# Single rows fetched by byte offsets kept in the sorted records, read 32 registers at a time, in a graph network kernel

## The reference, cut to what matters

```python
x = x + attention(h, src, dst, ...)
msg = xw[et_all, src_all]                       # layer 2: one of 8 x 12500 rows per edge and direction
out = sum over types of segment_sum(msg) * deg_inv + h @ self_weight
h2 = h[dst] + edge_attr_16 @ W_edge + b_edge    # layer 3, with the node itself as one more edge
agg = segment_sum(h2, src)
messages = (h @ W + b)[src] + edge_attr_6 @ We + be   # layer 4
x = x + relu(segment_sum(messages, dst))
```

## Time and profile before

| what | before |
|---|---|
| median of three timed runs | 21862.58 us |
| span of the profiled execution, first to last instruction | 15054.0 us |
| instructions in the span | 271220 |
| busy, of the span | GpSimd 74%, VectorE 65%, TensorE 58%, ScalarE 19% |
| HBM traffic over the span | 65 GB/s |

### The profile page before, as it was taken

The page is one execution under the profiler, slowest core; times in us unless marked ns, Lnnn a source line. Parts: engine busy times, 40 slices in busy tenths (PEclk is TensorE's granted clock), DMA queues, the critical chain, the costliest instruction groups (busy, mean ns, idle before and its releaser), DMA issues. The chain is left out here.

```text
span 15054.0 us, 271220 instructions
## 1 busy us (share of the span) xinstructions
PE 8740.4 (58%) x56159; PEld 6734.5 (45%) x56575; DVE 9778.7 (65%) x34050; ACT 2787.6 (19%) x7303; POOL 11087.4 (74%) x11347
## 2 busy tenths in 40 slices
PE   6766667777777777555555555555444444544444
PEld 2212226666666666244444444444333333433334
DVE  8877777777878778866666677777533333433334
ACT  0011114444444444421111111111100000200000
POOL 4777767777777777777777777777677777477776
PEclk8866668999999999865555555555555555655555
DMA  2011122222222222422222222222222222422222
GB/s 85 7 42 50 53 59 74 69 69 69 69 69 69 69 69 67 152 83 59 59 58 59 58 63 63 62 63 63 69 63 63 63 62 60 121 59 59 58 59 68
DMA packets 734382, 992.39 MB, mean 66 GB/s; under 512 B 271737, under 2 KB 534898, under 8 KB 732626
## 3 DMA queue, kind: packets, MB, share of 16 engines
q0 software_dynamic: 387968, 670.55, 17.1%
q1 hardware_dynamic: 324786, 301.13, 6.5%
q10 hardware_dynamic: 20000, 3.33, 0.1%
HBM read 795.25 MB, written 178.86 MB: 65 GB/s over the span
## 5 line engine op out<-in xcount | busy, mean ns | idle before, releaser
L1834 DVE TENSOR_TENSOR acc<-banks,acc 128x128 f32 x3328 | 969.8, 291 | 2616.2 <-PE banks L1792 2247.3
L668 POOL DMA_INDIRECT rec_dst<-stage_dst_sort,row_dst_sort x1563 | 1575.4, 1008 | 641.1 <-issue 474.3
L800 POOL DMA_INDIRECT far_att<-table_qv,recs_att x1664 | 1636.5, 983 | 523.9 <-issue 506.8
L800 POOL DMA_INDIRECT far_sum_dst<-table_h,recs_dst x1613 | 1561.2, 968 | 584.1 <-issue 491.7
L800 POOL DMA_INDIRECT far_sum_src<-table_h,recs_src x1613 | 1572.9, 975 | 558.8 <-issue 491.6
L800 POOL DMA_INDIRECT far_rel_src<-table_xw,recs_rel_src x1638 | 1574.7, 961 | 508.7 <-issue 494.2
L800 POOL DMA_INDIRECT far_rel_dst<-table_xw,recs_rel_dst x1638 | 1561.1, 953 | 510.4 <-issue 494.5
L1622 DVE TENSOR_TENSOR acc<-banks,acc 128x128 f32 x3328 | 969.7, 291 | 1119.2 <-PE banks L1548 1002.5
L936 POOL DMA_INDIRECT rec_src<-moved_att,row_src x1248 | 1245.0, 998 | 397.3 <-issue 379.9
L1792 PE MATMUL banks<-far_sum_src,hot_sum_src 128*128 128x128 f32 x3226 | 825.1, 436 | 1214.9 <-DVE hot_sum_src L1825 831.3
L1792 PE MATMUL banks<-far_sum_dst,hot_sum_dst 128*128 128x128 f32 x3226 | 825.9, 436 | 1147.5 <-DVE hot_sum_dst L1825 899.8
(11 more groups left out here) (343 smaller groups left out, 21302.0 us busy)
## 6 DMA issues: line engine op xcount, KB each, us to landing
lone_sync_rel_dst<-table_xw SPq DMA_DIRECT2D x3328, 0.5 KB
lone_sync_rel_src<-table_xw SPq DMA_DIRECT2D x3328, 0.5 KB
lone_sync_sum_src<-table_h SPq DMA_DIRECT2D x3328, 0.5 KB
lone_sync_sum_dst<-table_h SPq DMA_DIRECT2D x3328, 0.5 KB
lone_scalar_sum_src<-table_h ACTq DMA_DIRECT2D x3200, 0.5 KB
lone_scalar_sum_dst<-table_h ACTq DMA_DIRECT2D x3200, 0.5 KB
table_xw<-xw_rel_tables SPq DMA_DIRECT2D x98, 512.0 KB
far_att<-table_qv,recs_att POOLq DMA_INDIRECT x1664
```

What stands on the lines that cost most here:

```text
L668: e.indirect_dma_start(out=flat_dst, out_offset=bass.IndirectOffsetOnAxis(ap=row["dst"][:, c + i:c + i + 1], axis=0), in_=stage["dst"][:, ...
L800: e.indirect_dma_start(out=self.far[:, g % RING, t, :], out_offset=None, in_=table, in_offset=bass.IndirectOffsetOnAxis(ap=index, axis=0)) ...
L1834: e.tensor_tensor(acc[:, bass.ds(at[t], 1), :], sums[g0 % 4][:, t:t + 1, :], acc[:, bass.ds(at[t], 1), :], ALU.add).then_inc(k.s_sum, 1)
```

## The change

The records get two columns more, OFF and OFF8: IDX and IDX8 times 512, the byte where the row begins in its table. The column ONE goes, so a record has 12 and 22 columns. `staged` makes the two new columns with two ScalarE activations for each chunk and side. The fetching engine reads 32 offsets into 32 registers with one load, and a row's DMA takes its source from the table seen as a flat array of bytes, at the register's value. Blank records have offset 0. The buffers of row numbers and, in the relation passes, of the rows themselves lie in tensors whose use is over. ScalarE's rows in the sum passes are no longer fetched 128 at a time behind the copies: it goes through all groups and fetches 8 rows at each, with the copies at groups 16j + 5 and 16j + 10. Which tiles are fetched by row stays, but for one: ScalarE's first tile is now that of group 15, not 31.

```diff
-IDX, IDX8, LOC, TYP, ONE, ATT = range(6)
+IDX, IDX8, LOC, TYP, OFF, OFF8, ATT = range(7)
+ROW = F * 4
+LOAD = 32
...
             e.copy(to[:, b, 0:n, TYP], typ[:, c:c + n])
+            e.activation(to[:, b, 0:n, OFF].bitcast(I32), node[FAR[s]][:, c:c + n], ACT.Copy, scale=float(ROW))
+            e.activation(to[:, b, 0:n, OFF8].bitcast(I32), idx8[s][:, c:c + n], ACT.Copy, scale=float(ROW))
...
-    def fetch_rows(self, e, name, s, table, first, n):
-
-        for p in range(first, first + n, 8):
-            row = e.bass.values_load_multi_w_load_instructions(
-                self.ids[name][0:1, s % 2, p:p + 8], engines=[e.engine], min_val=0, max_val=table.shape[0] - 1,
...
-            for i in range(8):
-                e.dma_start(self.lone[name][p + i:p + i + 1, s % 2, :], table[bass.ds(row[i], 1), :]).then_inc(self.k.s_lone[name][s % 2], 16)
+    def single_rows(self, e, name, g, n, table, freed):
+
+        one = self.lone[name]
+        r, end = (min(P * h // one.step, P * len(one.groups)) for h in (g, g + n))
+        width = table.shape[1] * 4
+        flat = table.rearrange("n f -> (n f)").bitcast(U8)
+        while r < end:
+            s, first = divmod(r, P)
+            m = min(P - first, end - r)
+            if first == 0:
+                if s == 0:
+                    self.number_rows(e, name, 0)
+                if s >= 2:
+                    e.wait_ge(*freed(one.groups[s - 2]))
+                e.wait_ge(self.k.s_ids[name], self.ids_base[name] + 16 * (s + 1))
+                if s + 1 < len(one.groups):
+                    self.number_rows(e, name, s + 1)
+            for p in range(first, first + m):
+                if p % LOAD == 0:
+                    one.at = e.bass.values_load_multi_w_load_instructions(
+                        one.ids[0:1, s % 2, p:p + LOAD], engines=[e.engine], min_val=0, max_val=(table.shape[0] - 1) * width,
...
+                row = flat[bass.ds(one.at[p % LOAD], width)].rearrange("(a n) -> a n", a=1)
+                e.dma_start(one.buffer[p:p + 1, s % 2, :].bitcast(U8), row).then_inc(self.k.s_lone[name][s % 2], 16)
+            r += m
...
@@ relation_pass
-        lone, ids = {"sync": sb("lone_sync", [P, 2, F])}, {"sync": sb("ids_sync", [1, 2, P], I32)}
+        spent = [k.row_src[:, 2 * i * F:2 * (i + 1) * F].rearrange("p (b f) -> p b f", b=2) for i in range(2)]
+        lone = {"sync": Lone(spent[0].bitcast(F32), spent[1][0:1, :, :], OFF8, GT - 1, 15, 16)}
...
                 st.load(e, c)
                 if c:
-                    single_rows(c - 1)
-            single_rows(BLOCKS - 1)
+                    st.single_rows(e, "sync", (c - 1) * RG, RG, k.table_xw, freed)
+            st.single_rows(e, "sync", GROUPS - RG, RG, k.table_xw, freed)
...
@@ sum_pass, scalar
-            numbered = {1: st.number_rows(e, "scalar", 1, IDX)}
-            for j, (w0, n) in enumerate(WIN4):
-                b, m = j % 2, n * P
-                e.wait_ge(k.s_etr, f0 + j + 1)
...
-                st.fetch_rows(e, "scalar", s, k.table_h, 0, P)
+            for g in range(GROUPS):
+                j = beside(g, 5)
+                if j is not None:
+                    b, m = j % 2, WIN4[j][1] * P
+                    e.wait_ge(k.s_etr, f0 + j + 1)
...
+                j = beside(g, 10)
+                if j is not None and not gine:
...
+                st.single_rows(e, "scalar", g, 1, k.table_h, freed)
```

More of the change, by code:

```diff
@@ L766, in load_ahead, with __init__ @@
         e.dma_start(k.recs[s][:, c, :, :], k.rec[s][:, c * BT:(c + 1) * BT, :]).then_inc(k.s_rec[c], 16)
+class Lone:
+    def __init__(self, buffer, ids, column, tile, first, step):
+        self.buffer, self.ids, self.column, self.tile, self.step = buffer, ids, column, tile, step
+        self.groups = list(range(first, GROUPS, step))
+        self.at = None
 class Stream:
-    def __init__(self, k, s, recs, far=None, lone=None, ids=None):
-        self.k, self.rec, self.recs, self.far = k, k.rec[s], recs, far
-        self.lone, self.ids = lone or {}, ids
+    def __init__(self, k, s, recs, far, lone):
+        self.k, self.rec, self.recs, self.far, self.lone = k, k.rec[s], recs, far, lone
         self.rec_base, self.ring_base, self.lone_base = k.rec_base, list(k.ring_base), {n: list(b) for n, b in k.lone_base.items()}
+        self.ids_base = dict(k.ids_base)
     def load(self, e, c):
@@ L786, in fetcher @@
     def fetcher(self, g, t):
-        if g % LONE != LONE - 1:
-            return None
-        name = {GT - 1: "sync", GT - 2: "scalar"}.get(t)
-        return name if name in self.lone and (name == "sync" or g >= LONE) else None
+        for name, one in self.lone.items():
+            if t == one.tile and g in one.groups:
+                return name
+        return None
     def tiles(self, g):
@@ L807, in far_rows @@
         name = self.fetcher(g, t)
-        return self.lone[name][:, g // LONE % 2, :] if name else self.far[:, g % RING, t, :]
+        if name is None:
+            return self.far[:, g % RING, t, :]
+        one = self.lone[name]
+        return one.buffer[:, one.groups.index(g) % 2, :]
     def fetched(self, e, g):
@@ L834, in fetch_rows @@
-    def fetch_rows(self, e, name, s, table, first, n):
-        for p in range(first, first + n, 8):
-            row = e.bass.values_load_multi_w_load_instructions(
-                self.ids[name][0:1, s % 2, p:p + 8], engines=[e.engine], min_val=0, max_val=table.shape[0] - 1,
-                skip_runtime_bounds_check_because="the sort writes numbers of rows of the table alone")[1]
-            for i in range(8):
-                e.dma_start(self.lone[name][p + i:p + i + 1, s % 2, :], table[bass.ds(row[i], 1), :]).then_inc(self.k.s_lone[name][s % 2], 16)
+                s = self.lone[name].groups.index(g)
@@ new lines, in fetched, with number_rows @@
+                e.wait_ge(self.k.s_lone[name][s % 2], self.lone_base[name][s % 2] + 16 * P * (s // 2 + 1))
+    def number_rows(self, e, name, s):
+        one = self.lone[name]
+        tile = one.groups[s] * GT + one.tile
+        with self.k.nc.allow_non_contiguous_dma(reason="one number of each record"):
+            e.dma_start(one.ids[0:1, s % 2, :], self.rec[:, tile, one.column:one.column + 1].bitcast(I32).rearrange("p c -> c p")).then_inc(self.k.s_ids[name], 16)
+    def single_rows(self, e, name, g, n, table, freed):
+        one = self.lone[name]
+        r, end = (min(P * h // one.step, P * len(one.groups)) for h in (g, g + n))
[16 more added lines that the diff above has]
+                        one.ids[0:1, s % 2, p:p + LOAD], engines=[e.engine], min_val=0, max_val=(table.shape[0] - 1) * width,
+                        skip_runtime_bounds_check_because="the sort writes where rows of the table begin alone")[1]
+                row = flat[bass.ds(one.at[p % LOAD], width)].rearrange("(a n) -> a n", a=1)
+                e.dma_start(one.buffer[p:p + 1, s % 2, :].bitcast(U8), row).then_inc(self.k.s_lone[name][s % 2], 16)
+            r += m
@@ L849, in close @@
         self.k.rec_base += 16 * (BLOCKS // NREC)
-        if self.far is not None:
-            self.k.ring_base = [self.gathered(GROUPS - RING + r)[1] for r in range(RING)]
-        for name in self.lone:
+        self.k.ring_base = [self.gathered(GROUPS - RING + r)[1] for r in range(RING)]
+        for name, one in self.lone.items():
+            self.k.ids_base[name] += 16 * len(one.groups)
             for b in range(2):
-                self.k.lone_base[name][b] += 16 * P * self.turns(name, LONES - 2 + (LONES - 2 + b) % 2)
+                self.k.lone_base[name][b] += 16 * P * len(range(b, len(one.groups), 2))
 assert BLOCKS % NREC == 0 and GROUPS % RING == 0
@@ L1711, in sum_pass @@
         et = sb("et", [n_more, 2, G4 * P])
+        freed = lambda g: (k.s_product, p0 + g + 1)
         f0, bias0 = (0, 0) if gine else (len(WIN4), len(WIN4))
```

86 lines of the change are left out of this document (17 added, 69 removed).

## The result

| | before | after |
|---|---|---|
| time, median of 4 runs each | 21863.4 us | 20480.34 us |
| lowest and highest | 21862.25 to 21889.69 | 20478.82 to 20482.35 |
| ratio, 95% interval | | 0.9364 [0.9351, 0.9377] |
| profiled execution's time / span | not known / 15054.0 | 20478.82 / 20477.1 |

The change makes the kernel 6.4% faster, 1383 us. The forecast was 21864 us with a range from 21791 to 21941; it was wrong. The span of the profiled execution is its time less 1.7 us: nothing large lies outside the span.

What follows compares the result with a forecast made beforehand. The prediction took GpSimd's gathers, 1.265 us each, to bound the passes. It summed -2.5 (tiles) + 2.6 (staging) + 1 (longer records) = +1 us, giving 21864 us with 6808.6 us outside the span; range 21791 to 21941 us.

Steps and rivals of the forecast that it cites:

- the first one: Whole kernel: price the change in the 15054.0 us span; the 6808.6 us outside return only as a rival.
- the term at nothing: SyncE's block of rows in a pass: falls from 16.9 to 12.9 us, worth 0 on the pass's end.
- The cover: Passes with single rows: GpSimd's 19.9 us a block hides SyncE's; without it 4 us a block, 1.7 ms, would count.
- The rival nearest in number: Outside the span: 6808.6 us follow the instruction count, 25.1 ns each, so 1037 us less, 20830 us; chance 0.06.
- Gathers: GpSimd in the four passes: the bound, 1.265 us each; one tile less in each sum pass, -2.5 us.
- A row: SyncE's single rows: both register instructions go, leaving 0.28 us of 0.41 a row; bounds 0.28 and 0.41.
- The load of 32 registers: SyncE's register loads: 3.5 us for one wide load against 3.1 for four short ones; nothing won.
- ScalarE's second wait: ScalarE at group 16j + 10, last pass: 48 rows and two loads behind it, 21 us against 34, hidden, 0.
- Contention: Gathers in the four passes: lengthened or shortened by row traffic, taken as 0, bounds -73 to +70 us.
- the staging copies: Sort: two more ScalarE activations per chunk and side, about 0.26 us each, +2.6 us, from below 0 to 7.8.
- the longer records: Fills, scatters and loads: 9% and 5% more bytes, showing in each pass's first load, +1 us, between 0 and 3.
- The split row: Row DMAs: cut up, issue grows and SyncE becomes the bound over 0.50 us a row; +930 us, 22790; chance 0.05.

Runs made afterwards that it cites:

- e1: The kernel before, unedited, profiled once more: 15040.6 us where before took 15042.2, ratio 1.0001; its profiled execution took 15036.4 us with a span of 15034.7.
- e12: The kernel before, unedited, run again for its trace in a session where before took 21880.8 us: 21897.3 us, ratio 1.0004.
- e14: The changed kernel with row numbers in the registers, so a product at each row again: 21989.3 us where before took 21880.8, ratio 1.0046.
- e2: The changed kernel with row numbers in the registers, so a product at each row again: 15012.1 us where before took 15042.2, ratio 0.9981.
- e15: The changed kernel with no single rows, SyncE issuing waits on a long reached value instead: 19860.9 us where before took 21880.8, ratio 0.9079.
- e4: The changed kernel with no single rows, every tile a gather of GpSimd: 15239.7 us where before took 15042.2, ratio 1.0130.
- a1: The changed kernel, unedited, timed beside the kernel before: 15037.8 us where before took 15064.5, ratio 0.9985.
- e5: The changed kernel with each row fetched by two DMAs of 256 B: 17896.8 us where before took 15064.5, ratio 1.1879.

## Why the prediction was wrong

**The step that failed** is the first one, as put there: "the span is 15054.0 us, 6808.6 us less than the median of the timed runs ... what lies outside comes back as a rival", and in the sum "with 6808.6 us outside as in the median". From it followed the term at nothing, "On the end of the pass this is worth 0". Nothing lies outside: the span is the time less 1.7 to 1.8 us in after, in e1 and in e12. The 6808.6 us were thus no measurement of what lies around a kernel, as one rival took them. The time was inside, as pauses and what waits for them, in executions other than the profiled one. A page whose span is 69% of the timed median is a page of other conditions, and its covers could not be taken to hold. That should have had the weight of a rival, with the price from my own text.

**The cover.** "On the end of the pass this is worth 0. The cover is GpSimd's 19.9 us; if it were gone, 4 us a block in 416 blocks, 1.7 ms, would count." It was gone: drawn out, SyncE's block in before is 28.4 us and GpSimd's, 23.8, no longer hides it. The passes gave back 1413 us, 3.4 us a block. The mechanism and even the size stood in the text, at no chance. The size isn't all luck: the pauses stay about what they were, and calm the block fell from 16.9 to 12.7 us, 4.2. But its two terms were off in opposite ways, as the list below says.

**The rival nearest in number**, the time follows the number of instructions (20830, chance 0.06), was right that fewer instructions pay, and wrong in place and price. They pay within the span, and where their queue is the bound: e14 puts back 13312 on SyncE and 6656 on ScalarE for 1491 us drawn out, the same edit costs nothing calm (e2), and e15's 26024 recorded waits cost 272 us in the passes. That 20830 lies near 20480 is luck.

**In a calm session the forecast held**, -27 us where it said +1, within 0.2%. By its terms:
- Gathers: 1638 and 1612, median 944 ns, 0.3 us between. The bound was named rightly; e4 confirms 1.265 us a gather.
- A row: said 0.28 us, measured 10.23 / 32 = 0.32 in a1's timeline. Only FUSED_REGOPS went, the MOVE of 29 ns stayed.
- The load of 32 registers: said 3.5 us, measured 2.06, 65 ns a register where eight take 98 each. There is a fixed part, which I had dismissed; "Nothing is won by the wide load" was wrong by 1 us a block, and hidden.
- The two errors cancel: block 0.4 + 2.1 + 10.2 = 12.7 us for 12.9, wait 6.4 us for 6.5. That the block came out right is luck.
- ScalarE's second wait was set against 34 us; the six groups behind it give 6 x 4.9 = 29, still over the 21 needed.
- Contention: the four groups are busy 6257 us where the earlier trace rows add up to 6270, -13 us, inside its bounds. ScalarE's rows, the staging copies and the longer records show in no stage.
- The split row didn't happen: a row issues in 228 ns, and SyncE's queue has 324786 packets as before. e5, at 0.75 us a row, shows what the rival would have meant, a bound on SyncE; nothing here tests its 0.50 us closely.

**Open.** What draws executions out. It held for whole sessions, calm in two and drawn out in three here. It goes with GpSimd's indirect DMAs: the stage between the sum passes, which has none, takes 158 us in after and 160 in before's calm trace. The stage that fills the tables takes 714 us in after and 451 in a1, and cut where the last scatter ends it reads (columns as above):

```profile
8817.00:9239.00 422.00, 85.54 (x156) 39.78 (x156) 124.30 (x274) 61.94 (x149) 319.33 (x314) 0.57 0.22 68
9239.00:9531.00 292.00, 189.04 (x530) 94.85 (x530) 215.87 (x539) 148.64 (x411) 0.99 (x2) 0.85 0.40 150
```

While GpSimd scatters, TensorE gets 156 products done in 422 us; after it, 530 in 292. In a1 all 686 are done beside the scatters in 440 us. The records of semaphore events thin out at the same time: the relation pass dst has some 8900 landings recorded in after and 34200 in a1. The Trainium skill, page "NOTIFIC — the notification-queue block", section "Overflow: three behaviours, one of which stalls the engine", says that this block's inner pipeline always holds back its producers rather than lose a record. By that rule the pauses could be the recording's own. Pauses at any instruction would fit it; the landings that are missing don't decide it, as the rule speaks only of the inside of the block. Every run here has a recorded span, so it wasn't tried without, and no run here shows it.

## What to carry to other kernels

Compare the profiled execution's span with the timed median before anything else. Here the two differ by 1.7 to 1.8 us where both are of one execution; if they differ by thousands, the page shows other conditions than the runs do, and each "hidden: 0" needs a chance of its own for the cover being gone. Where one queue issues a long stream of small instructions beside the bound, cut instructions from it even when it is covered: here it was worth nothing calm and 6.4% drawn out. The room gained has opposite uses in the two cases: more rows by SyncE (every twelfth group, 0.993) calm, fewer (every 32nd, 0.890, or none, 0.885) drawn out. Both beat both kernels where they belong; no version was best in both.

## What the runs showed of the hardware

- The kernel before took 15042 and 21881 us in two sessions, with all its runs of a session within 0.5% of each other.
- Drawn out, register moves, products, satisfied waits and DMA issues all pause, mostly for about 0.7 us or twice that, while their medians stay 29, 37, 28 and 220 to 228 ns. An indirect DMA of GpSimd keeps its 947 ns. The pauses add some 11 us to a block of SyncE's rows, with 101 instructions in it or with 66.
- A register load on SyncE, calm, has a fixed part: 781 ns for 8 registers, 2064 for 32, (2064 - 781) / 24 = 53 ns for each further one and some 350 fixed.
- A row of 512 B with a register in its address costs SyncE 0.32 us calm, a product for its address 0.096 more, and two DMAs of 256 B with an ALU_OP for the second's address 0.75.
